# Four heads of a cross-attention in four row strips of the array: scores, exponents, values and mask of a Flamingo block

## The reference

```python
scores = jnp.einsum('bhqd,bhkd->bhqk', Q, K) * scale      # 4 x 16 x 256 x 1601, head dimension 8
scores = jnp.where(mask, -jnp.inf, scores)                # layer 3 only
attn = jax.nn.softmax(scores, axis=-1)
ctx = jnp.einsum('bhqk,bhkd->bhqd', attn, V)
```

## Time and profile before

| what | value |
|---|---|
| median of 3 runs | 2006.02 us (2004.76 to 2010.19) |
| the profiled execution | span 2004.8 us from first to last instruction, mean granted clock 0.949 |
| TensorE matmul busy | 1839.7 us, 92% |
| VectorE busy | 1427.8 us, 71% |
| ScalarE busy | 1217.7 us, 61% |
| DMA | 58 GB/s mean |

### The profile page before, as it was taken

One profiled execution on the slowest core, in us unless ns is written; L12 is line 12 of the kernel. 1 busy time (PEld: TensorE's weight loads), 2 busy tenths in 40 slices (PEclk: granted clock), 3 DMA queues, 4 the chain that ended last, 5 costly groups with the idle time before them and its releaser, 6 DMA issues.

```text
span 2004.8 us, 43706 instructions
## 1 busy us (share of the span) xinstructions
PE 1839.7 (92%) x14449; PEld 800.7 (40%) x14449; DVE 1427.8 (71%) x2650; ACT 1217.7 (61%) x2194; POOL 146.3 (7%) x239
## 2 busy tenths in 40 slices
PE   6699999977779999997897999999789999999978
PEld 4333333345222333333574233333344444444445
DVE  6688888647878888883685888888457666666448
ACT  3177777742435777775793577777534566565636
POOL 5000000012000000002121000000000000000012
PEclk9899999989998999998898899999988999999979
DMA  9711111105111111110115111111051111111001
GB/s 259 231 36 51 36 52 35 59 1 171 35 44 45 44 44 43 44 35 22 43 54 174 44 45 44 44 44 35 33 174 36 36 35 35 35 35 35 20 6 38
DMA packets 78783, 116.81 MB, mean 58 GB/s; under 512 B 16823, under 2 KB 50958, under 8 KB 78702
## 3 DMA queue, kind: packets, MB, share of 16 engines
q1 hardware_dynamic: 75326, 106.84, 17.9%
q0 software_dynamic: 2432, 7.94, 1.3%
q10 hardware_dynamic: 944, 0.93, 0.1%
HBM read 81.12 MB, written 34.23 MB: 58 GB/s over the span
## 4 chain that ended last, share of the span: by engine, by line
PE 82%; DVE 8%; ACT 3%; DMA 3%; issue 2%; POOL 1%; SPq 1%; DVEq 0%; ACTq 0%; POOLq 0%
PE pv_bank L1420 23%; PE exp_ring L1402 22%; PE score_ring L1389 18%; PE exp_ring L1406 5%; DVE mx L997 3%; PE score_ring L1566 3%; PE exp_ring L1577 3%; DMA k_d<-k2c 2%; PE score_ring L1331 1%; ACT early L771 1%; PE exp_ring L1338 1%; PE score_ring L1479 1%; DMA qp<-ms 1%; DVE stats L913 1%; PE score_ring L1370 1%
## 5 line engine op out<-in xcount | busy, mean ns | idle before, releaser
L771 ACT ACTIVATE early<-exp_ring 128x512 f32<-128x512 f32 (+1 forms) x1728 | 970.7, 596 | 485.1 <-PE exp_ring L1402 303.1
L997 DVE TENSOR_REDUCE mx<-score_ring 128x1 f32<-128x800 f32 (+2 forms) x896 | 784.5, 907 | 163.2 <-PE score_ring L1389 151.2
L1402 PE MATMUL exp_ring<-qp,kp 128*128 128x512 f16 (+1 forms) x1728 | 623.1, 387 | 7.3 <-DMA qp<-ms 6.9
L1389 PE MATMUL score_ring<-kp,qp 128*128 128x400 f16 (+2 forms) x2176 | 573.8, 345 | 43.3 <-DVE mx L997 22.9
L1420 PE MATMUL pv_bank<-early,vg 128*32 128x256 f32 (+1 forms) x6912 | 555.1, 391 | 1.8 <-ACT o_all L760 0.9
L1402 PEld LDWEIGHTS exp_ring<-qp,kp 128*128 128x128 f16 (+1 forms) x1728 | 149.2, 98 | 397.1 <-ACT early L771 279.8
L1389 PEld LDWEIGHTS score_ring<-kp,qp 128*128 128x128 f16 x2176 | 208.8, 99 | 238.8 <-DVE mx L997 86.0
L1420 PEld LDWEIGHTS pv_bank<-early,vg 128*32 128x32 f32 (+1 forms) x6912 | 139.2, 108 | 270.3 <-issue 157.8
L1406 PE MATMUL exp_ring<-mask_eye,mask 128*128 128x256 f16 (+1 forms) x832 | 159.2, 273 | 0.0
L1406 PEld LDWEIGHTS exp_ring<-mask_eye,mask 128*128 128x128 f16 (+1 forms) x832 | 82.3, 99 | 59.0 <-issue 0.7
L607 POOL COPY vg<-v_all 128x416 f32 (+1 forms) x48 | 25.4, 533 | 1030.6 <-PE pv_bank L1420 983.1
(11 more groups left out here) (231 smaller groups left out, 1162.7 us busy)
## 6 DMA issues: line engine op xcount, KB each, us to landing
kp<-k_d SPq DMA_DIRECT2D x128, 400.2 KB, 3.1
k_d<-k1c SPq DMA_DIRECT2D x32, 400.2 KB, 7.0
ctxT<-ctxT_d SPq DMA_DIRECT2D x12, 800.5 KB, 6.2
k_d<-k2c SPq DMA_DIRECT2D x16, 400.2 KB, 7.6
qp<-q_d SPq DMA_DIRECT2D x320, 12.0 KB
k_d<-v_loc POOLq DMA_DIRECT2D x12, 400.2 KB, 9.2
ctxT_d<-ctxT SPq DMA_DIRECT2D x4, 800.5 KB, 7.4
o_all<-in_ctx SPq DMA_DIRECT2D x4, 768.0 KB
```

Source lines behind the costliest of these rows:

```text
L771: act.activation(pt[g][0:rows_, 2 * h:2 * h + 2, :], bank[0:rows_, :].rearrange("p (i q) -> p i q", q=S), ACT.Exp).then_inc(exped, 1)
L997: dve.tensor_reduce(dst, src, AX.XY, ALU.max).then_inc(score_free, 1)
L1389: ins = pe.matmul(pa[slot][:, z, 0:w], qp1[par][:, i, qt * P:qt * P + P], kp1[par][:, at:at + w], start=True, stop=True)
L1402: ins = pe.matmul(bank[0:rows_, :], kp2[par][:, s * P:s * P + rows_], qp2[par][:, 2 * h:2 * h + 2, :], start=True, stop=True, skip_group_c ...
```

## The change

Each matmul of the two passes now uses only one head's rows of the array, at that head's partitions.

- **Scores.** The stationary operand is Q of one head, 24 rows x 128 queries, so `qp1` is one tile of 128 x 256 and needs no zeros between heads and one DMA instead of four. Without a mask a piece is now two heads (0 and 1, or 2 and 3) and one chunk of 400 or 401 keys, one head per bank; with a mask it stays one head and two chunks. There are 16 pieces as before (4 instead of 8 in the local run, each of two heads).
- **Maxima.** They are kept as one f16 row (row 24 of each head's strip). VectorE writes them straight into `m16`, 128 columns wide and zero elsewhere; TensorE transposes it (now 128 x 128) and VectorE adds the result to `qp1` into `qp2` in one operation. The copy L1029, two small VectorE operations and the DMA `qp<-ms` are gone. SyncE starts the loads of unit n+2 after that addition, no longer after the copy.
- **Exponents.** A fill is one head and two key tiles: two matmuls of 256 columns, both in the same row strip, into one bank. There are 28 fills per unit (7 pairs of key tiles x 4 heads, the last pair half empty) instead of 26.
- **Product.** It runs once per pair of key tiles: 7 times per unit instead of 13, with the same matmuls.
- **Mask.** It is transposed once at the start (26 transposes, 7 copies by ScalarE) and added by one 128-row matmul of 512 columns ahead of each fill's two.
- **Start.** GpSimd writes zeros over the unused rows of `q_d` with 16 more DMAs.

```diff
-KM = KQ + 2
+KM = KQ + 1
...
-        qp1 = [sb(f"qp1_{i}", [P, HG, S], F16) for i in range(2)]
+        qp1 = [sb(f"qp1_{i}", [P, S], F16) for i in range(2)]
...
             def pass1(r, n, par):
                 sp.dma_start(kp1[par][:, 0:r.nk], k_d[r.index][n]).then_inc(in1[par], 16)
-                for i in range(HG):
-                    sp.dma_start(qp1[par][R * i:R * i + KQ, i, :], q_d[r.layer][n, R * i:R * i + KQ, :]
-                                 ).then_inc(in1[par], 16)
+                sp.dma_start(qp1[par][:, :], q_d[r.layer][n]).then_inc(in1[par], 16)
...
-                    sp.wait_ge(q_kept, r.u0 + n + 1)
+                    sp.wait_ge(score_free, FREE_SCORE + r.turn_use(n) + 1)
...
+                    for q in q_d:
+                        for b in range(B):
+                            pool.dma_start(q[4 * b:4 * b + 4].rearrange("g (i r) n -> (g i) r n", r=R)[:, KQ:R, :],
+                                           zero16[:, :]).then_inc(q_zero, 16)
...
-                def keep_rows(par, slot, use):
+                def shift_rows(par, slot, use):
 
                     dve.wait_ge(score, use + 1)
-                    dve.tensor_copy(ms[par][:, :], pa[slot][:, 0, :].bitcast(F16)[0:2 * HG, 0:S]
-                                    ).then_inc(score_free, 1)
+                    dve.tensor_tensor(qp2[par][:, :], pa[slot][:, 0, :].bitcast(F16)[:, 0:S], qp1[par][:, :], ALU.add
+                                      ).then_inc(score_free, 1)
...
-                    qt, c, i = j // (cpt * HG), j // HG % cpt, j % HG
-                    lo, w, nb = r.chunks[c]
-                    for z in range(nb):
-                        at = lo + z * (S2 // 4)
-                        ins = pe.matmul(pa[slot][:, z, 0:w], qp1[par][:, i, qt * P:qt * P + P],
-                                        kp1[par][:, at:at + w], start=True, stop=True)
+                    qt, banks = r.banks_of(j)
+                    for z, (i, c) in enumerate(banks):
+                        at, w = r.chunks[c]
+                        ins = pe.matmul(pa[slot][:, z, 0:w], qp1[par][R * i:R * i + KQ, qt * P:qt * P + P],
+                                        kp1[par][R * i:R * i + KQ, at:at + w], start=True, stop=True)
                     ins.then_inc(score, 1)
...
-                    ins = pe.matmul(bank[0:rows_, :], kp2[par][:, s * P:s * P + rows_],
-                                    qp2[par][:, 2 * h:2 * h + 2, :], start=True, stop=True, skip_group_check=r.mask)
                     if r.mask:
-                        for qt in range(QT):
-                            ins = pe.matmul(bank[0:rows_, :].rearrange("p (i q) -> p i q", q=S)[:, :, qt * P:qt * P + P],
-                                            mask01[:, qt, s * P:s * P + rows_],
-                                            mask_eye[:, :].unsqueeze(1).broadcast_to([P, 2, P]),
-                                            start=False, stop=True, skip_group_check=True)
+                        pe.matmul(bank[0:rows_, 0:two * S], mask_eye[0:rows_, 0:rows_],
+                                  maskT[0:rows_, 2 * sp_:2 * sp_ + two, :].rearrange("p k q -> p (k q)"),
+                                  start=True, stop=False, skip_group_check=True)
+                    for z, s in enumerate(r.tiles(sp_)):
+                        ins = pe.matmul(bank[0:rows_, z * S:z * S + S], kp2[par][R * h:R * h + KM, s * P:s * P + rows_],
+                                        qp2[par][R * h:R * h + KM, :], start=not r.mask, stop=True,
+                                        skip_group_check=r.mask)
```

## The result

The changed kernel takes 2603.3 us (median of 4 runs, 2602.85 to 2608.65) against 2005.68 for the kernel before: a ratio of 1.2976, 95% interval 1.2953 to 1.3000. Forecast were 1940 us and a range of 1850 to 2010. The profiled execution has a span of 2606.9 us and a mean granted clock of 0.598; before it was 0.949.

What follows compares the result with a forecast made beforehand. The prediction took TensorE, busy 92% of the span, as the bound. From 2004.8 us it took 105 for units without mask and 10 for the local run, added 46 for mask and 4 for preparation: 1940 us, range 1850 to 2010.

Steps and rivals of the forecast that it cites:

- Pairs side by side, 0.18: Score matmuls on TensorE: two in different row strips run together, 0.18 us per pair instead of 0.34.
- Rival B: Score pairs: row strips do not run side by side; 2036 us, slower; chance 0.13.
- The unit without mask, 17.3: Long runs without mask: a unit takes 17.3 us instead of 19.9, bounds 16.3 and 18.6; three runs gain 105 us.
- rival C: Units without mask: pieces waiting for VectorE stall TensorE's in-order queue; 19.2 us per unit, 2015 in all; chance 0.12.
- the two loops: Units without mask: fills and exponents through three banks give 16.9 us; score pieces waiting for VectorE's slots add 0.4.
- the one of 0.4 us for VectorE: Units without mask: uneven score pieces wait for VectorE's slots and hold fills behind them, 0.4 us added per unit.
- Changes of row shape, 0.10: Masked run: switching TensorE between all rows and one strip costs 0.10 us, 49 times per unit, 4.9 us.
- the mask at 28.5: Layer 3: a masked unit takes 28.5 us against 25.6, including 4.9 for shape changes less 0.9 for overlap; +46 us.
- Rival A: Masked run: changing row shapes is free; 23.5 us per unit, 1863 us in all; chance 0.20.
- Local run, 4.7: Local run: a loop through the load of unit n+2 takes 4.7 us per unit against 5.3; -10 us.
- Preparation, +4: Start of the kernel: mask transposes and copies hidden, 16 more DMAs cost time; +4 us, ends 0 and +8.

Runs made afterwards that it cites:

- 64-row run: Strips of 64 rows instead of 32 in both passes, score pairs of heads 0 and 2 or 1 and 3, against the changed kernel: 2029.05 us.
- the product early and `PAUSE` 0: Rows chosen by run, product after a group's third fill, no empty places between two units' score pieces, against the changed kernel: 1942.55 us.
- the versions above: Changed kernel with 24/25 rows in the local run, 64 in long unmasked runs, 128 in the masked: 1973.23 us; with later order and local-run edits, down to 1912.43.

## Why the prediction was wrong, by its own steps

**The step that failed** is one that the prediction took without naming it as a step: every duration came from rows at clock 1.00, and 1.00 was kept for matmuls on 24 and 25 rows, of which no row existed. No rival had another clock either. The clock was 0.50, and a unit without mask became 27.3 us instead of 17.3, one with mask 41.7 instead of 28.5; with all rows back, 560 of the 598 us of loss were gone. A bound from both sides was owed here as much as for the row strips, and would have put a time far above 2010 into view.

The Trainium skill ("TensorE: Matmul & The Clock Gate", Part 1, What's actually happening) ties the gate to how busy TensorE has been. The rows above don't bear that out by busy time: layer 3 is busy 499.70 of 500.00 us at a mean clock of 0.58, and the 64-row run is busy 214.46 of 240.00 at 1.00. Here the measurement decides.

**Pairs side by side, 0.18: right.** 0.52 us for two at clock 0.50, 0.37 at 1.00. Rival B, the slower one, did not happen; the result was slower for a reason outside all three rivals.

**The unit without mask, 17.3: right in kind, mis-sized.** At clock 1.00 it measured 18.7, just above the upper bound of 18.6 and between the forecast and rival C's 19.2. TensorE's work per unit was 16.7 us where 16.3 was forecast, and it stood 2.0 where the two loops were given 1.0. The term most short is the one of 0.4 us for VectorE: in the 64-row run TensorE waited in 120 to 360 us 9.8 + 2.5 us on VectorE's maxima (ahead of score pairs, and of the transposes), 1.0 us per unit, and 6.1 on ScalarE:

```profile
PE score_ring L1435 <- DVE mx L1033: 9.8, 25, 0.6
PE exp_ring L1455 <- ACT early L798: 6.1, 13, 0.5
PE score_ring L1416 <- DVE mx L1033: 2.5, 13, 0.3
```

With the product early and `PAUSE` 0 it is 18.1 to 18.2, so 0.5 of the 1.4 us was order. The rest was not separated.

**Changes of row shape, 0.10, and the mask at 28.5: right.** 28.3 at clock 1.00. In the 64-row run's layer 3 a fill starts 0.32 us behind its mask matmul, and the next mask matmul 0.32 behind the fill, where 0.215 would be the columns alone:

```profile
1701.57 0.39 PE L1455 MATMUL exp_ring<-qp2f,kp 64*128 64x256 f16 x2
1701.89 0.39 PE L1450 MATMUL exp_ring<-maskT,mask_eye 128*128 128x512 f16 x1
1702.21 0.39 PE L1455 MATMUL exp_ring<-qp2f,kp 64*128 64x256 f16 x2
```

In the kernel before with 24-row scores some 30 changes made 2.5 us, 0.08 each. Rival A (free) is out: with all 128 rows, where the changes are gone, the same layer takes 24.9, as 28.5 less 4.9 plus 0.9 leads one to expect (24.5). The Trainium skill ("TensorEngine Tiling (Array Packing)", Key Properties under Tiling Modes) states that a change of mode drains the engine; these rows agree and give the price.

**Local run, 4.7: right in the number, in part by luck.** Starts of first fills in the changed kernel:

```profile
655.19 0.60 PE L1440 MATMUL exp_ring<-qp,kp 25*128 25x256 f16 x2
...
659.60 0.60 PE L1440 MATMUL exp_ring<-qp,kp 25*128 25x256 f16 x2
```

4.4 us, even at clock 0.50: 0.9 less than before instead of 0.6. But the forecast's 4.7 was a loop through the load, in which TensorE needed only 3.1. In the changed kernel TensorE is busy 37.64 of the 40 us from 640 to 680 and waits for no load: at half the clock its own work nearly fills the unit. In the versions above the same run took 6.4 to 6.8 us with four loads, 5.4 with one, and 4.5 with one load, one addition and the product where the changed kernel has it.

**Preparation, +4:** the first reduction of scores starts at 79.97 us, against 77.47: +2.5.

**Small slips in the sums.** Rival B without its 0.9 has 29.4 us per masked unit, not 29.6, and +58 us by the forecast's own count, so 2030 instead of 2036. Span and time were taken as one; the time is 1.7 us above the span in the changed kernel (2608.65 and 2606.9). Neither decides anything.

Put together, at clock 1.00 in the long runs the forecast of 1940 would still have been missed. The 64-row run took 2029, of which its own loads and additions in the local run explain some 32 (its local unit is 6.4 us, 16 x 2.0), so by 57 to 89 us, and 1.4 us in each of 42 units is 59 of them. Whether the kernel had become faster or slower would have hung on the mask's rows: 28.3 against 24.9 us per unit is 54 us.

## What to carry to other kernels

A tiling that makes each matmul occupy fewer rows can lose the clock, and then everything on TensorE pays: before costing such a change by rows of the trace, ask whether any of them has a matmul of that shape, and carry the lower clock as a rival until one run has shown it. Rows filled with zeros cost TensorE nothing here (a score matmul of 401 columns reads 0.334 us on 128 rows and 0.336 on 64) and kept the clock in the long runs; where row strips are worth having, try the widest that still run side by side (64 here), and all rows where whole-array matmuls stand between them. When a unit gets shorter, the order that was right for the old one must be tried again: one constant was worth 27 us here and minus 20 there.

## What the runs showed of the hardware that was not expected

- Matmuls on 24 and 25 rows leave the granted clock at 0.50 with TensorE busy 88% of the time in layer 0; on 64 rows it is 1.00 at 89%; on 32 rows the same loop shows 0.50 for 180 us, then 0.94 for 20, then 0.50 again.
- In the steady loop of layer 0 one of two interleaved passes on all rows was enough: clock 1.00 with the other at 24 or 25. It was not enough at the start of a run (0.50 with TensorE busy 40.00 of 40.00 us) nor in the local run (0.50).
- Not only score pairs, but a fill and a score pair in different strips start together (301.87 and 301.88), through different instructions and into different banks.
- A single change of row shape costs some 0.10 us, in either direction, at clock 1.00 and at 0.50.
